# A macaron block on one core: pair sums for the group score, convolution taps on ScalarE and GpSimd, a router of eight products

## The reference

```python
x = x + 0.5 * ffn(layernorm(x))     # x: 16 sequences x 256 positions x 128 features, float32
x = x + attn(layernorm(x))
x = x + 0.5 * ffn(layernorm(x))

def ffn(tokens):
    scores = sigmoid(tokens @ router_weight.T)                # 32 experts
    sfc = scores + router_bias
    grp = sfc.reshape(T, 4, 8)
    group_scores = top_k(grp, 2)[0].sum(-1)                   # the two best of each group of 8
    keep = the 2 best of the 4 groups
    idx = top_k(where(keep, sfc, 0.0), 4)
    w = 2.5 * scores[idx] / (scores[idx].sum() + 1e-20)
    experts = silu(tokens @ gate_w[e].T) * (tokens @ up_w[e].T) @ down_w[e].T     # inner size 64
    return sum over idx of w * experts + one shared expert of inner size 128

def attn(x):
    gate, val = split(x @ W_in.T)
    v = depthwise convolution of val over 5 positions + conv_b
    y[t] = tanh(a_param) * y[t - 1] + sigmoid(gate[t]) * v[t]
    res = x + y @ W_out.T
    return layernorm(res) * ln_w + ln_b
```

## Time and profile before

| | |
|---|---|
| median of 3 runs | 672.98 us (671.9 to 673.3) |
| the profiled execution | 672.07 us |
| its span, first to last instruction | 670.3 us |
| granted TensorE clock over the span | 1.000 |
| busy, share of the span | TensorE 98%, VectorE 82%, GpSimd 67%, ScalarE 63% |

### The profile page before, as it was taken

One profiled execution on the slowest core, in us unless ns is written; L12 is line 12 of the kernel. 1 busy time (PEld: TensorE's weight loads), 2 busy tenths in 40 slices (PEclk: granted clock), 3 DMA queues, 4 the chain that ended last, 5 costly groups with the idle time before them and its releaser, 6 DMA issues. The chain is left out here.

```text
span 670.3 us, 10334 instructions
## 1 busy us (share of the span) xinstructions
PE 656.8 (98%) x3083; PEld 530.8 (79%) x3083; DVE 548.9 (82%) x1540; ACT 420.7 (63%) x804; POOL 446.5 (67%) x452
## 2 busy tenths in 40 slices
PE   8899999999999999999999999999999999999997
PEld 7787888888888887888888888888878778777675
DVE  5888889979878877879879898788979868867765
ACT  4756666675676656766476755767676566655554
POOL 2346667866776766766677775867676776776564
PEclk9999999999999999999999999999999999999999
DMA  9664909248091925629084470917419074380561
GB/s 223 144 142 99 188 11 226 51 110 162 26 224 42 215 53 124 133 80 206 17 187 101 108 147 22 227 41 168 104 32 223 2 172 100 75 181 17 118 137 32
DMA packets 60232, 78.30 MB, mean 117 GB/s; under 512 B 8176, under 2 KB 27664, under 8 KB 60176
## 3 DMA queue, kind: packets, MB, share of 16 engines
q1 hardware_dynamic: 59600, 77.63, 52.2%
q10 hardware_dynamic: 576, 0.02, 0.1%
HBM read 74.49 MB, written 3.15 MB: 116 GB/s over the span
## 5 line engine op out<-in xcount | busy, mean ns | idle before, releaser
L576 POOL TENSOR_TENSOR hid_lo<-hid,hid_hi 128x512 fp32r<-128x512 f32 x270 | 348.3, 1294 | 188.3 <-ACT hid_hi L689 188.0
L840 DVE TENSOR_TENSOR weighted<-gate_ps,raw 128x512 f32<-128x512 f32 x256 | 175.2, 684 | 69.7 <-ACT gate_ps L681 64.1
L681 ACT ACTIVATE gate_ps<-gate_ps 128x512 f32<-128x512 f32 x256 | 148.7, 581 | 119.7 <-PE gate_ps L1119 116.4
L689 ACT ACTIVATE hid_hi<-hid 128x512 fp32r<-128x512 f32 x272 | 170.4, 626 | 64.4 <-DVE hid L853 61.1
L853 DVE TENSOR_TENSOR hid<-weighted,up_ps 128x512 f32<-128x512 f32 x256 | 174.3, 681 | 8.0 <-issue 0.5
L1190 PE MATMUL down_ps<-hid_lo,wt_hi 128*128 128x512 f32 x272 | 108.0, 397 | 0.2 <-DVE hid_lo L861 0.2
L1187 PE MATMUL down_ps<-hid_hi,wt_hi 128*128 128x512 f32 x272 | 107.8, 396 | 0.0
L1188 PE MATMUL down_ps<-hid_hi,wt_lo 128*128 128x512 f32 x272 | 107.7, 396 | 0.0
L1117 PE MATMUL gate_ps<-xT_hi,wt_hi 128*128 128x512 f32 x170 | 72.0, 423 | 0.0
L1117 PE MATMUL up_ps<-xT_hi,wt_hi 128*128 128x512 f32 x170 | 68.4, 402 | 2.4 <-DVE hid L853 2.3
L1118 PE MATMUL gate_ps<-xT_lo,wt_hi 128*128 128x512 f32 x170 | 67.3, 396 | 0.0
(11 more groups left out here) (187 smaller groups left out, 1108.4 us busy)
## 6 DMA issues: line engine op xcount, KB each, us to landing
raw<-wT_hbm SPq DMA_DIRECT2D x96, 512.0 KB, 11.6
raw<-wT_hbm SPq DMA_DIRECT2D x62, 256.0 KB, 4.5
x_ln<-in_L_attn_x SPq DMA_DIRECT2D x8, 256.0 KB, 4.0
x_res<-in_L_attn_x SPq DMA_DIRECT2D x8, 256.0 KB, 3.7
out_x<-x SPq DMA_DIRECT2D x7, 256.0 KB, 2.3
raw<-in_L_ffn_gate_w SPq DMA_DIRECT2D x4, 256.0 KB, 4.9
raw<-in_L_ffn_up_w SPq DMA_DIRECT2D x4, 256.0 KB, 4.9
raw<-in_L_ffn_down_w SPq DMA_DIRECT2D x4, 256.0 KB, 5.2
```

The costliest lines, as they stand in the source:

```text
L576: nc.gpsimd.tensor_tensor(hid_lo[s][:, :], hid[s][:, :], hid_hi[s][:, :].bitcast(F32), ALU.subtract)\
L681: nc.scalar.activation(bank[:, :] if j else silu_sb[:, :], bank[:, :], ACT.Silu).then_inc(silu_done, 1)
L689: nc.scalar.activation(hid_hi[s][:, :], hid[s][:, :], ACT.Copy).then_inc(hid_hi_done, 1)
L840: V.tensor_tensor(weighted[j % 2][:, :], gate_ps[n % BANKS][:, :], wb[:, j - 1, :], ALU.mult)\
```

## The change

Three parts.

**Router.** The high and the low weights now lie in one tile `wt`, and one product of 64 columns gives high by high and high by low side by side. The low by high product of 32 columns is added to the first half. That makes 8 products for 12. The first step of the routing on VectorE adds the halves (`raw_logit`).

**Group score.** The steps 5 to 13 are replaced: the sum of the two best of eight is the largest of seven sums, 4 pair sums of the eight values, 2 of the larger ones of the pairs, 1 of the two left. `biased` moves from PSUM to SBUF, `pair_sum`, `top_half`, `top_quarter` and `gsum_by_group` are in SBUF. The comparison of the groups is laid out otherwise. The chain has 25 steps for 26; the logits that silu waits for are step 3 now, not 2.

**Convolution.** `conv` is gone from VectorE. ScalarE makes each tap as a product with a scalar into one of two SBUF tiles, GpSimd adds them up in the SBUF tile `value`, four additions a block. VectorE keeps the gate and the recurrence, which now read `value` from SBUF, and come later. The tables are changed for it.

```diff
-        side_te = side_td[:, :, 0:E]
+        side_te = side_td[:, :, 0:2 * E].rearrange("p t (h e) -> p t h e", h=2)
...
-        biased = routed[:, 128:256].rearrange("p (t e) -> p t e", t=TT)
+        biased = sb("biased", [P, TT, E])
...
```

```diff
         ADD = {"copy ffn 1": 1, "transpose ffn 1": 4, "add ffn 1": 8.5}
         PROJECT = {"stats 2": 1.5, "meanvar 2": 2, "norm 2": 2, "normalise 2": 3, "transpose 2": 9, "xT high 2": 9,
                    "xT low 2": 9.5, "mixer gate": 10, "tanh gate": 10, "mixer value": 12, "copy value": 12,
-                   "add ln_b": 16}
+                   "tap": (13, 14, 15, None), "add tap": (15, 16, None, None)}
...
-        MIXER = {"conv": (0, 0, 0, 0, 0.5, 1.5), "y high": 5, "y low": 5, "mixer out": 9, "mixer sum": 12.5,
+        MIXER = {"tap": (None, None, None, 1), "add tap": (None, None, 0, 2), "gate value": 3, "recur": 3.5,
+                 "add ln_b": 9, "y high": 5, "y low": 5, "mixer out": 9, "mixer sum": 12.5,
                  "stats 3": 13}
```

```diff
+            def add_tap(b, part):
+
+                if part == 0:
+                    pool.wait_ge(first_tap_done, b + 1)
+                else:
+                    pool.wait_ge(tap_added, b * TAPS + part)
+                pool.wait_ge(tap_done, b * TAPS + part + 1)
+                nc.gpsimd.tensor_tensor(value[:, :], value[:, :], tap_of[part % 2][:, :], ALU.add)\
+                  .then_inc(tap_added, 1)
...
                 nc.scalar.activation(wT[k][:, :], side[:, 0:P], ACT.Copy).then_inc(wT_done[k], 1)
+
+            def tap(b, part):
+
+                act.wait_ge(mix_val_done, b + 1)
+                if b * TAPS + part >= 2:
+                    act.wait_ge(tap_added, b * TAPS + part - 1)
+                nc.scalar.activation(tap_of[part % 2][:, :].rearrange("p (s t) -> p s t", s=SB),
+                                     val_pad[:, :, part + 1:part + 1 + SEQ], ACT.Copy,
+                                     scale=taps_half[:, part + 1:part + 2]).then_inc(tap_done, 1)
```

```diff
                 if n == 0:
                     dve.wait_ge(logits_ready[k], b + 1)
-                    return st.done(V.tensor_scalar(tiny[:, :, :], logits, -1e-9, 1e-8, ALU.is_ge, ALU.mult))
-                if n == 3:
+                    return st.done(V.tensor_reduce(raw_logit[:, :, :], logits.rearrange("p t h e -> p t e h"),
+                                                   AX.X, ALU.add))
+                if n == 4:
                     dve.wait_ge(logit_silu_done[k], b + 1)
-                st.wait()
+                if n not in (7, 9):
+                    st.wait()
                 if n == 1:
-                    st.done(V.tensor_tensor(logit[:, :, :], tiny[:, :, :], logits, ALU.add))
+                    st.done(V.tensor_scalar(tiny[:, :, :], raw_logit[:, :, :], -1e-9, 1e-8, ALU.is_ge, ALU.mult))
                 elif n == 2:
+                    st.done(V.tensor_tensor(logit[:, :, :], tiny[:, :, :], raw_logit[:, :, :], ALU.add))
+                elif n == 3:
                     st.done(V.reciprocal(logit_inv[:, :, :], logit[:, :, :]))
-                elif n == 3:
+                elif n == 4:
                     st.done(V.tensor_tensor(score[:, :, :], logit_silu[:, :, :], logit_inv[:, :, :], ALU.mult))
-                elif n == 4:
+                elif n == 5:
                     st.done(V.tensor_tensor(biased[:, :, :], score[:, :, :],
                                             bias_b[:, :].unsqueeze(1).broadcast_to([P, TT, E]), ALU.add))
-                elif n == 5:
-                    st.done(V.tensor_reduce(per_group(best1), by_group(biased), AX.X, ALU.max))
                 elif n == 6:
-                    st.done(V.tensor_tensor(by_group(is_best), by_group(biased), over_group(best1), ALU.is_equal))
+                    st.done(V.tensor_tensor(pair_sum[:, :, 0:HALF], grouped(biased)[:, :, 0:HALF],
+                                            grouped(biased)[:, :, HALF:PG], ALU.add))
                 elif n == 7:
-                    st.done(V.scalar_tensor_tensor(others[:, :, :], is_best[:, :, :], FAR, biased[:, :, :],
-                                                   ALU.mult, ALU.add))
+                    st.done(V.tensor_tensor(top_half[:, :, :], grouped(biased)[:, :, 0:HALF],
+                                            grouped(biased)[:, :, HALF:PG], ALU.max))
                 elif n == 8:
-                    st.done(V.tensor_reduce(per_group(n_best), by_group(is_best), AX.X, ALU.add))
+                    st.done(V.tensor_tensor(pair_sum[:, :, HALF:HALF + QUARTER], top_half[:, :, 0:QUARTER],
+                                            top_half[:, :, QUARTER:HALF], ALU.add))
                 elif n == 9:
-                    st.done(V.tensor_reduce(per_group(best_other), by_group(others), AX.X, ALU.max))
+                    st.done(V.tensor_tensor(top_quarter[:, :, :], top_half[:, :, 0:QUARTER],
+                                            top_half[:, :, QUARTER:HALF], ALU.max))
                 elif n == 10:
-                    st.done(V.tensor_scalar(far_single[:, :], n_best[:, :], 1.5, FAR, ALU.is_lt, ALU.mult))
+                    st.done(V.tensor_tensor(pair_sum[:, :, PAIRS - 1], top_quarter[:, :, 0], top_quarter[:, :, 1],
+                                            ALU.add))
                 elif n == 11:
-                    st.done(V.tensor_tensor(best1_tied[:, :], far_single[:, :], best1[:, :], ALU.add))
+                    st.done(V.tensor_reduce(gsum[:, :, :].rearrange("p t g -> p (t g)"), pair_sum[:, :, 0:PAIRS],
+                                            AX.X, ALU.max))
                 elif n == 12:
-                    st.done(V.tensor_tensor(best2[:, :], best1_tied[:, :], best_other[:, :], ALU.max))
+                    st.done(V.tensor_copy(gsum_by_group[:, :, :], gsum[:, :, :].rearrange("p t g -> p g t")))
...
+                    st.done(V.tensor_tensor(gdiff.rearrange("p h (t g) -> p h t g", t=TT),
+                                            gsum_by_group[:, :, :].unsqueeze(3).broadcast_to([P, NG, TT, NG]),
+                                            gsum[:, :, :].unsqueeze(1).broadcast_to([P, NG, TT, NG]),
+                                            ALU.subtract))
...
+            def gate_value(i):
+
+                dve.wait_ge(tap_added, i * TAPS + TAPS)
                 dve.wait_ge(mix_gate_done, i + 1)
-                st.wait()
...
+                V.scalar_tensor_tensor(value[:, :], gate_t[:, :], 1.0, value[:, :], ALU.add, ALU.mult)\
+                 .then_inc(gated, 1)
+
+            def recur(i):
+
+                dve.wait_ge(gated, i + 1)
                 if i > 0:
                     dve.wait_ge(y_lo_done, i)
-                st.done(V.tensor_tensor_scan(y[:, :], decay[:, :], mixed[:, :], 0.0, ALU.mult, ALU.add))
-                assert st.n == MIX
+                V.tensor_tensor_scan(y[:, :], decay[:, :], value[:, :], 0.0, ALU.mult, ALU.add).then_inc(mix, 1)
```

```diff
                 pe.wait_ge(xT_lo_done[k], b + 1)
-                w_hi, w_lo = wt_hi[:, WROUTER, 0:E], wt_lo[:, WROUTER, 0:E]
+                w_hi = wt_hi[:, WROUTER, 0:E]
                 for t in range(TT):
                     rows = slice(t * P, (t + 1) * P)
-                    x_hi, x_lo = hi_of(k, b)[:, rows], lo_of(k, b)[:, rows]
-                    nc.tensor.matmul(side_te[:, t, :], x_hi, w_hi, start=True, stop=False)
-                    nc.tensor.matmul(side_te[:, t, :], x_hi, w_lo, start=False, stop=False)
-                    last = nc.tensor.matmul(side_te[:, t, :], x_lo, w_hi, start=False, stop=True)
+                    nc.tensor.matmul(side_te[:, t, :, :], hi_of(k, b)[:, rows], wt[:, :, WROUTER, 0:E],
+                                     start=True, stop=False)
+                    last = nc.tensor.matmul(side_te[:, t, 0, :], lo_of(k, b)[:, rows], w_hi, start=False, stop=True)
```

165 lines of the change are left out of this document (75 added, 90 removed), and 1 row of the table END.

## The result

| | before | after |
|---|---|---|
| median | 672.98 us (671.8 to 673.5, 5 runs) | **737.02 us** (735.6 to 738.6, 5 runs) |
| ratio | | 1.096 (95%: 1.094 to 1.098) |
| span of the profiled execution | 670.3 us | 735.6 us |
| mean granted TensorE clock | 1.000 | 0.980 |

What follows compares the result with a forecast made beforehand. TensorE, 98% busy, was taken as the bound. Fifteen units losing 1.5 us each, router gain included, add 22.5 to 672.07, less 0.8 in the set-up: 693.8; on the median 694.7, stated as 695 us, range 664 to 711.

Steps and rivals of the forecast that it cites:

- Router: TensorE's router: four products fewer give 0.45 us a router, 16 x 0.45 = 7.2 us in all.
- Set-up: Set-up before the units: earlier logits and a shorter routing chain cut TensorE's wait for w_tok, 0.8 us gained.
- Port waits of the chain: VectorE's routing chain: two-SBUF-input operations each wait 0.41 us for GpSimd, 7 x 0.41 = 2.9 us more a chain.
- the 1.35 and 1.6: Forecast losses of units (4, 1) and (1, 5), in us, with the router's gain already in them.
- ScalarE's taps lie in its idle time (it is busy 63%): ScalarE: 32 taps of 783 ns at most fit its idle time; the later wT copy costs nothing, or 1.6 us in two units.
- The gate and the recurrence: On VectorE, reading value from SBUF: 0.8 us more over a pair of units.
- the unit (1, 5): The gate waits for the last addition, then hid_lo 2, to 312.65; tile 6's up product 1.2 us later, 1.6 in all.
- The mean of two middle units: Mean of 1.35 and 1.6, 1.5 us, taken for all fifteen units with a routing chain: 22.5 us.
- The covers: GpSimd's lateness stays hidden: hid_lo 16 done at 306.3, down product needs it at 307.58, 1.3 us left.
- Take turns throughout: Rival: chain operations between weighted and hid all wait to a hid_lo's end; 2.5 us a unit, 710 us, chance 0.13.
- Waits that fit the slack: Rival: waits stay below 1.25 us and 3 us in the two stretches, only gains remain; 664 us, chance 0.24.
- that cancel: Rival: a wait of 0.5 us a unit beyond the slack against the router's 0.45; 672 us, chance 0.05.

Runs made afterwards that it cites:

- e6: The whole change with the routing tiles in PSUM and upper halves in small SBUF tiles, two tap buffers kept; 716.7 us, ratio 1.067.
- e3: The change with the convolution, gate, recurrence and tables as before, so router and pair sums only, in SBUF; 693.2 us, ratio 1.031.
- e5: e3 with the routing tiles in PSUM and the upper halves again in three small SBUF tiles; 670.15 us, ratio 0.9975.
- e7: e4 with the routing tiles in PSUM as in e5; 697.5 us, ratio 1.038.
- e4: The change with four tap tiles where it had two, so ScalarE never waits for an addition within a block; 720.9 us, ratio 1.073.
- e10: e7 with gate_t and the gated value in the PSUM bank mixed; 687.2 us, ratio 1.023.
- e15: e10 with gate, recurrence and y in later slots, recurrence always behind hid, early blocks' taps one a slot; 675.24 us, ratio 1.0055.
- e8: The kernel before with the router of eight products alone, raw_logit in PSUM; 670.66 us, ratio 0.9979.
- e14: e13 with ScalarE's four taps a block also cut to one column; 677.7 us.
- e13: e10 with later gate, recurrence and y slots, early blocks' taps one a slot, and GpSimd's additions cut to one column; 678.3 us.

## Why the prediction was wrong

The loss, put together from the differences of the runs above (they are from several chips, on which the kernel before takes 671.6 to 673.0 us):

| | us |
|---|---|
| port waits of the routing (after to e6; 23 from e3 to e5) | 20.3 |
| waits for a tap tile in ScalarE's list (e6 to e7; 16 from after to e4) | 19.2 |
| gate and recurrence: port waits (e7 to e10) | 10.3 |
| slots of taps, gate, recurrence, y (e10 to e15) | 12.0 |
| not resolved but for 2.1 of GpSimd's additions (e15 over e5) | 5.1 |
| router and pair sums without port waits (e5 against before) | -2.8 to -1.7 |

The size of a row depends on the order in which the causes are taken away (later slots give 11.2 us ahead of e10 and 6.7 behind it); their sum does not. So a row is what a remedy gave at its turn, and not always what the change itself lost by that cause: in the change the gate waits for the port in four blocks (1.73 to 1.76 us), but in the three middle ones it takes 0.68, where it takes 1.75 to 1.77 in e7.

- *Router.* Right in its size: the slot with the router takes 2.91 us for 3.35 and 2.21 for 2.66 in e8, 0.44 less. Wrong in its worth: of the 7.2 us e8 keeps 1.2. In a middle pair of units one of the two 0.44 comes back two slots on (3.15 us become 3.53); why is not shown.
- *Set-up.* 0.8 us forecast; the first `hid` of the program starts at 20.68 for 21.73, 1.05.
- *Port waits of the chain.* Right in the mechanism and near in size, in part by luck. I had 2.9 us more a chain than in before. Over the ten operations concerned, the means of e3 less those of e5 come to 3.0; 0.42 of them are `gdiff`'s own, which before had too, so 2.6 are new, and 0.56 of these are `tiny` and the copy, which my sum left out: what it did count came to 2.0. e3, where this is nearly the whole change, took 693.2, and a middle pair of its units 2.9 us more than before, for 3.0 forecast. But the two units of the pair are 2.2 and 0.7, not the 1.35 and 1.6 that I added up, and the 1.6 had the gate in it, which e3 leaves where it was: two errors cancel. And the 695 were meant for the convolution too. TensorE's wait for `hid` was to be some 25 us and is 16.1.
- **"ScalarE's taps lie in its idle time (it is busy 63%)" is the step that failed.** I costed the taps by ScalarE's busy share and never asked what a tap itself waits for. The wait for `tap_added` stood in the diff; the first addition is in slot 15 of a GpSimd that does "norm 4" in slot 14 and runs behind. What is queued behind the third tap is silu, `hid_hi` and `normed`. That is 28.4 us of waiting, 16 us (e4) to 19 us (e7) of time, and it had no place in the sum or among the rivals. By itself it does not bring the time into the range (e4 takes 720.9 for at most 711); the next two steps failed as well. The taps' own time is free, as I had it: e14 is 0.6 us under e13, less than the spread of either.
- *The gate and the recurrence.* I gave the two 0.8 us a pair. Their port waits cost 10 us in e7, and their slots a part of the 12.0 above. The waits are on the gate alone: in the change it takes 1214 ns for the 687 of e3, the recurrence 1210 for 1213. Nor did the unit (1, 5) go as I had it. There the gate waits neither for the last addition nor for a port; `tiny`, just ahead of it, has waited for the `hid_lo` that ends at 341.40. The 4.9 us of waiting for the last addition, in five blocks, all lie in units of the ends. The two rows of the unit (1, 5):

```profile
340.93 0.56 DVE L932 TENSOR_SCALAR tiny<-raw_logit 128x128 f32<-128x128 f32 x1
341.41 0.68 DVE L1008 SCALAR_TENSOR_TENSOR value<-gate_t,value 128x512 f32<-128x512 f32 x1
```

- *The mean of two middle units stood for all fifteen.* A middle pair takes 5.7 us more than before, for 3.0 forecast; with four tap tiles (e4) it is 3.7, so 2.0 are the tap wait, and 0.7 more the rest of the convolution. The six middle units lose 18 us together, the nine others 47. For the routing the mean was good even there (e3 loses 1.4 us a unit in the middle and 1.5 elsewhere), for the convolution it was not. The units at both ends have tables of their own, with two taps in a slot or a gate right behind the last addition, and there three units went from 40.1 to 51.3, from 42.7 to 52.3 and from 39.8 to 47.3 us. I never read them.
- *The covers.* GpSimd's lateness hardly reaches the down product: the one wait for GpSimd's `hid_lo` that the profile shows is that of the weight load, 1.2 us in three places. VectorE's wait for the weights to come back grew from 5.3 to 9.5 us, but it is 8.4 in e5, which has no taps on ScalarE, so the later `wT` is not what made it.
- *The clock.* Not in the forecast: at most 14.7 us at a mean of 0.980, 2 us at e3's 0.997. It adds to the cost of some long stops.
- *The rivals.* "Take turns throughout" (710) was nearest by number and not by cause. Waits that fit the slack, or that cancel, are out: only with the routing tiles in PSUM does any gain appear.

## What to carry to other kernels

Before work is moved to an engine with idle time, write down for each moved instruction what it waits for and what stands behind it in that engine's list: an engine that is 63% busy can still hold up everything behind one wait, and a second pair of buffers is the cheap test (16 us here). Beside a busy GpSimd an operation on VectorE took its own time here if it read at most one SBUF tile and, for `tiny` and the copy, if its input was in PSUM; an operand in PSUM brought `top_half` from 631 to 223 ns. And a slot table has rows for the ends of the program: cost those apart, and put a long operation behind the one that TensorE waits for, never ahead.

The version that beats both kernels is e5 (670.15 us, 0.25% under before, interval 0.16 to 0.35%): the router of eight products and the pair sums with their tiles in PSUM, the convolution left alone. But e8, the router alone, is at 670.66 with an interval that overlaps e5's (0.12 to 0.30% under before), so no gain of the pair sums over the old group score is shown.
